# Cross attention with each step's projection piece ahead of its turn, VectorE's order changed to match, and the first norm moved into the loading block

## The reference, cut to what matters

```python
def _L0_attn_ref(x, ...):
    h = _ln(x, g1, beta1)                       # the "first norm"
    q = _phi((h @ wq).reshape(b, s, H, DH), proj)
    k = _phi((h @ wk).reshape(b, s, H, DH), proj)
    v = (h @ wv).reshape(b, s, H, DH)
    ...                                          # causal linear attention, wo, FFN
def _L0_xattn_ref(x, context, ...):
    xn = layer_norm(x, ...); cn = layer_norm(context, ...)
    q, k, v = xn @ Wq, cn @ Wk, cn @ Wv          # 16 heads of 64
    sim = einsum('bhid,bhjd->bhij', q * scale, k)     # 112 x 375 for each head
    attn = softmax(where(mask, sim, neg))
    out = einsum('bhij,bhjd->bhid', attn, v) @ Wo
x = _layernorm(x + _L0_attn_ref(x, ...))
x = _layernorm(x + _L0_xattn_ref(x, ctx, ...))
x = _layernorm(x + _L0_ffn_ref(x, ...))
```

## Time and profile before

| | |
|---|---|
| median of 3 runs | 2275.87 us |
| profiled execution, its own time | 2277.0 us |
| its span, first to last instruction | 2275.3 us |
| mean granted TensorE clock | 0.982 |
| busy: PE, PEld, DVE, ACT, POOL | 96%, 72%, 67%, 61%, 34% |
| layer 1, cross attention, layer 3 | to about 770, 770 to 2000, from 2000 us |

### The profile page before, as it was taken

How to read it: one execution, slowest core, us unless ns; L and a number is a source line. 1 busy time by engine, 2 the same in 40 slices (tenths; PEclk the granted TensorE clock), 3 DMA queues, 4 the chain that set the end, 5 groups by cost and what they waited for, 6 DMA issues and landing times. The chain is left out here.

```text
span 2275.3 us, 57835 instructions
## 1 busy us (share of the span) xinstructions
PE 2182.2 (96%) x20778; PEld 1640.8 (72%) x20778; DVE 1519.3 (67%) x4396; ACT 1380.3 (61%) x3178; POOL 762.4 (34%) x1335
## 2 busy tenths in 40 slices
PE   5999999999998999999999999999999999989997
PEld 4766867867867667777777777767677777868886
DVE  4555445545547677777777777777777777465647
ACT  5556356356354476767676767676767676544534
POOL 1122212212215244545444445454545454200003
PEclk8999999999999999999999999999999999789999
DMA  4100000000001100000000000000000000043202
GB/s 133 47 1 1 0 0 0 0 0 0 15 0 57 35 16 10 16 10 16 10 16 10 16 11 15 12 14 13 13 14 12 16 3 2 1 113 112 74 1 65
DMA packets 45732, 51.44 MB, mean 23 GB/s; under 512 B 19120, under 2 KB 37664, under 8 KB 45504
## 3 DMA queue, kind: packets, MB, share of 16 engines
q1 hardware_dynamic: 45504, 48.45, 7.2%
HBM read 44.78 MB, written 3.67 MB: 21 GB/s over the span
## 5 line engine op out<-in xcount | busy, mean ns | idle before, releaser
L1727 POOL TENSOR_SCALAR arena<-arena,p_rec 112x375 f32<-112x375 f32 x512 | 304.6, 596 | 617.3 <-DVE p_rec L1593 616.9
L64 PE MATMUL b_pb<-arena 128*125 128x512 f16 (+1 forms) x1364 | 379.9, 299 | 1.5 <-DVE k_lo L1564 1.5
L66 PE MATMUL b_pb<-arena 128*125 128x512 f16 (+1 forms) x1364 | 377.5, 298 | 0.0
L65 PE MATMUL b_pb<-arena 128*125 128x512 f16 (+1 forms) x1364 | 377.1, 297 | 0.0
L1597 DVE TENSOR_TENSOR pt_lo<-b_t,pt_hi 125x336 f16<-125x336 f32 x512 | 256.5, 501 | 140.7 <-ACT pt_hi L1488 140.7
L1579 DVE CUSTOM_DVE_ANT_0 arena<-b_s,arena 112x375 f32<-112x375 f32 x512 | 275.0, 537 | 100.6 <-PE b_s L1339 87.4
L1482 ACT ACTIVATE arena<-arena,neg_max 112x375 f32<-112x375 f32 x512 | 308.1, 602 | 1.4 <-DVE neg_max L1579 1.4
L1488 ACT ACTIVATE pt_hi<-b_t 125x336 f16<-125x336 f32 x512 | 226.9, 443 | 107.3 <-PE b_t L1348 107.2
L1348 PE MATMUL b_t<-ident,arena 112*125 112x112 f32 x1536 | 274.9, 288 | 12.3 <-POOL arena L1727 12.3
L1348 PEld LDWEIGHTS b_t<-ident,arena 112*125 112x125 f32 x1536 | 215.9, 190 | 71.0 <-POOL arena L1727 27.3
L952 POOL TENSOR_SCALAR_AFFINE_SELECT sm<-sm 112x448 f32<-112x448 f32 x128 | 72.0, 586 | 420.9 <-ACT sm L632 420.9
(11 more groups left out here) (279 smaller groups left out, 5726.0 us busy)
## 6 DMA issues: line engine op xcount, KB each, us to landing
arena<-in_L_ffn_W_dram SPq DMA_DIRECT2D x16, 1024.0 KB, 7.4
arena<-in_ctx_dram SPq DMA_DIRECT2D x32, 375.0 KB
out_dram<-c_z SPq DMA_DIRECT2D x8, 448.0 KB, 3.2
x_sb<-in_x_dram SPq DMA_DIRECT2D x1, 3136.0 KB, 18.8
ff<-in_L_attn_w_dram SPq DMA_DIRECT2D x2, 1024.0 KB, 6.8
ff<-in_L_xattn_Wkv_dram SPq DMA_DIRECT2D x2, 1024.0 KB, 5.3
arena<-in_mask_BxS_bf_dram SPq DMA_DIRECT2D x32, 41.0 KB, 2.6
a_raw<-in_L_attn_wq_dram SPq DMA_DIRECT2D x1, 1024.0 KB, 5.1
```

What stands on the lines that cost most here:

```text
L64: pe.matmul(out, lh, rh, start=first, stop=False)
L65: pe.matmul(out, lh, rl, start=False, stop=False)
L66: return pe.matmul(out, ll, rh, start=False, stop=last)
L1727: pool.tensor_scalar(p32[:, h % 4, :], p32[:, h % 4, :], p_rec[:, h % 4:h % 4 + 1], 0.0, ALU.mult, ALU.add).then_inc(p_norm_done, 1)
```

## The change

In cross attention the piece goes ahead of the turn on TensorE, and `piece_high` ahead of `turned_high` on ScalarE. On VectorE `turned_low` moves behind `sum_reciprocal`, and on odd steps behind `mask_max` as well. The last sequence, which has no pieces, keeps its order on TensorE and ScalarE. In the loading block x moves ahead of wk in the SyncE queue, wq and wk get semaphores of their own so that the transposes of wq need not wait for wk, and statistics, reciprocal root and rows of the first norm are made there.

```diff
 # layer1, main block, vector:
-            for b in range(G4):
-                ln_stats(0, b, x_rows(0)).then_inc(stats_done[0], 1)
-            ln_moments(0, 0)
-            for b in range(G4):
-                ln_rows(0, 0, b, x_rows(0), xh_rows)
             ln_low(0, 0)
             split_low(0)
 # layer1, main block, gpsimd:
-            ln_rstd(0, 0)
             pool.memset(v1[:, :, :, 0:DH], 0.0).then_inc(pads_done, 1)
 # load_layer1, sync:
             for i, n in enumerate(("L0_attn_wq", "L0_attn_wk")):
-                sp.dma_start(raw[i][:, :, :], rows(a[n])).then_inc(raw_loaded, 16)
+                sp.dma_start(raw[i][:, :, :], rows(a[n])).then_inc(raw_loaded[i], 16)
+                if i == 0:
+                    sp.dma_start(x_sb[:, 0:G4, :], ...).then_inc(x_loaded, 16)
             sp.wait_ge(p2_zero, 1)
...
-            sp.dma_start(x_sb[:, 0:G4, :], ...).then_inc(x_loaded, 16)
...
-            sp.wait_ge(x_loaded, 16)
 # load_layer1, gpsimd, behind ident:
+            settle(pool, passed, (mom_done, 1))
+            pool.tensor_scalar(rstd[:, 0, :], mom[:, 0, :, 1], EPS, None, ALU.add).then_inc(eps_done, 1)
+            pool.wait_ge(eps_done, 1)
+            pool.tensor_tensor(rstd[:, 0, :], rstd[:, 0, :], half_neg[0:T, :], ALU.pow).then_inc(rstd_done, 1)
 # load_layer1, tensor:
-            pe.wait_ge(raw_loaded, 32)
             for n in range(NT):
                 w, m2 = divmod(n, KI // 2)
+                if m2 == 0:
+                    pe.wait_ge(raw_loaded[w], 16)
 # load_layer1, vector, ahead of the fold's low parts:
+            dve.wait_ge(x_loaded, 16)
+            for b in range(G4):
+                dve.bn_stats(stats[:, 0, b, :], x_sb[:, b, :]).then_inc(stats_done, 1)
+            settle(dve, passed, (stats_done, G4))
+            for b in range(G4):
+                ins = dve.bn_aggr(mom[:, 0, b, :], stats[:, 0, b, :])
+            ins.then_inc(mom_done, 1)
+            dve.wait_ge(rstd_done, 1)
+            for b in range(G4):
+                ins = dve.tensor_scalar(xh[:, b, :], x_sb[:, b, :], mom[:, 0, b, 0:1], rstd[:, 0, b:b + 1], ALU.subtract, ALU.mult)
+            ins.then_inc(rows_done, 1)
 # layer2, tensor:
                 for s in range(H):
-                    turn_scores(b, s)
                     if not is_last(b):
                         piece(b + 1, 1 - par, s)
-                    else:
+                    turn_scores(b, s)
+                    if is_last(b):
 # layer2, scalar:
-                    turned_high(b, s)
                     if not is_last(b):
                         piece_high(b + 1, 1 - par, s)
-                    else:
+                    turned_high(b, s)
+                    if is_last(b):
 # layer2, vector:
-                    turned_low(b, s)
                     if s + 2 < H:
                         sum_reciprocal(b, s + 2)
                     elif not is_last(b):
                         sum_reciprocal(b + 1, s + 2 - H)
+                    if s % 2 == 0:
+                        turned_low(b, s)
                     if s + AHEAD < H:
                         mask_max(b, par, s + AHEAD)
                     elif not is_last(b):
                         mask_max(b + 1, 1 - par, s + AHEAD - H)
+                    if s % 2 == 1:
+                        turned_low(b, s)
```

More of the change, by code:

```diff
@@ L191, in layer1 @@
         b2 = sb("a_b2", [T, D], F32)
-        load_layer1(nc, a, x_sb, ident, half_neg, consts_done, hi, lo, (g1, be1, g2, be2, b1, b2), sb_in, psum_in, sem)
+        LNS = 3
+        xh = sb("xh", [T, G4, D], F32)
+        stats = sb("a_stats", [T, LNS, G4, 6], F32)
+        mom = sb("a_mom", [T, LNS, G4, 2], F32)
+        rstd = sb("a_rstd", [T, LNS, G4], F32)
+        norm_sems = [[sem(f"a_{n}{i}") for i in range(LNS)] for n in ("stats_done", "mom_done", "eps_done", "rstd_done", "rows_done")]
+        load_layer1(nc, a, x_sb, ident, half_neg, consts_done, hi, lo, (g1, be1, g2, be2, b1, b2),
+                    (xh, stats, mom, rstd), [sems[0] for sems in norm_sems], passed, sb_in, psum_in, sem)
         def pair(name, k, c0, n, width):
@@ L199, in layer1 @@
         FT = FF // P
-        LNS = 3
         NSM = 4
-        xh = sb("xh", [T, G4, D], F32)
         h32 = sb("h32", [P, KD, GT], F32)
@@ L222, in layer1 @@
         late = ("wv", "wo", "w1", "w2")
-        stats = sb("a_stats", [T, LNS, G4, 6], F32)
-        mom = sb("a_mom", [T, LNS, G4, 2], F32)
-        rstd = sb("a_rstd", [T, LNS, G4], F32)
         NPB = 4
@@ L347, in layer1 @@
         pb_free = [sem(f"a_pb_free{i}") for i in range(NPB)]
-        stats_done, mom_done, eps_done, rstd_done, rows_done = (
-            [sem(f"a_{n}{i}") for i in range(LNS)] for n in ("stats_done", "mom_done", "eps_done", "rstd_done", "rows_done"))
+        stats_done, mom_done, eps_done, rstd_done, rows_done = norm_sems
         h_hi_done = [sem(f"a_h_hi_done{i}") for i in range(2)]
@@ L1034, in _, with load_layer1 @@
             ln_rstd(NG - 1, 2)
-def load_layer1(nc, a, x_sb, ident, half_neg, consts_done, hi, lo, vectors, sb_in, psum_in, sem):
+def load_layer1(nc, a, x_sb, ident, half_neg, consts_done, hi, lo, vectors, norm, norm_sems, passed, sb_in, psum_in, sem):
     stack = ExitStack()
@@ L1042, in load_layer1 @@
         g1, be1, g2, be2, b1, b2 = vectors
+        xh, stats, mom, rstd = norm
+        stats_done, mom_done, eps_done, rstd_done, rows_done = norm_sems
         raw = [sb(f"a_raw{i}", [P, KD, INNER], F32) for i in range(2)]
@@ L1047, in load_layer1 @@
         fold_ps = [psum(f"a_fold{i}", [P, 4 * P]) for i in range(4)]
-        raw_loaded, vec_loaded, x_loaded = sem("a_raw_loaded"), sem("a_vec_loaded"), sem("a_x_loaded")
+        raw_loaded = [sem(f"a_raw_loaded{i}") for i in range(2)]
+        vec_loaded, x_loaded = sem("a_vec_loaded"), sem("a_x_loaded")
         p2_zero, p2_loaded = sem("a_p2_zero"), sem("a_p2_loaded")
@@ L1058, in _ @@
             for i, n in enumerate(("L0_attn_wq", "L0_attn_wk")):
-                sp.dma_start(raw[i][:, :, :], rows(a[n])).then_inc(raw_loaded, 16)
+                sp.dma_start(raw[i][:, :, :], rows(a[n])).then_inc(raw_loaded[i], 16)
+                if i == 0:
+                    sp.dma_start(x_sb[:, 0:G4, :], a["x"][0:G4, :, :].rearrange("b t d -> t b d")).then_inc(x_loaded, 16)
             sp.wait_ge(p2_zero, 1)
@@ L1062, in _ @@
                 sp.dma_start(proj2[DH * r:DH * (r + 1), DH * r:DH * (r + 1)], a["L0_attn_proj"]).then_inc(p2_loaded, 16)
-            sp.dma_start(x_sb[:, 0:G4, :], a["x"][0:G4, :, :].rearrange("b t d -> t b d")).then_inc(x_loaded, 16)
             for t, n in ((g1, "g1"), (be1, "beta1"), (g2, "g2"), (be2, "beta2"), (b1, "b1")):
```

## The result

The changed kernel takes 2253.23 us (median of four, 2248.58 to 2260.7) against 2276.03 for the kernel before: ratio 0.9887, 95% interval 0.986 to 0.9914. That is 22.8 us, where 39 had been forecast; it lies inside the range of 2222 to 2260 and on the side that had the chance of 0.93.

The account below looks back on a forecast made before the run. TensorE, busy 196.9 of 200 us in cross attention, was taken to set the pace. Loop -26 (-0.87 in thirty sequences), layer's first turn -2.2 and beginning -11.4 made -39.6 from 2277.0; forecast 2237 us, range 2222 to 2260.

Parts of the forecast that it names:

- The beginning and the layer's first turn: Loading block: first turn and first phi sooner, -11.4 us; layer's first turn: a piece fills its GpSimd wait, -2.2 us.
- The turn of step 8: Cross attention, TensorE: a piece covers the wait for GpSimd's normalise and the turn is no longer cold, -0.60 us a sequence.
- The seven other cold turns: Cross attention, TensorE: turns behind scores or values now stand behind a piece, -0.35 us a sequence (0 to -0.70).
- Scores behind a turn: Cross attention, TensorE: eight scores start sooner behind a turn than behind a piece, 0.02 us each, -0.16 a sequence.
- Scores that wait for mask_max: Cross attention, step 2: VectorE's turned order on odd steps brings the mask 0.4 us forward, -0.21 us a sequence.
- (b): VectorE: pieces 11 and 12 need piece_low of 9 and 10; just fits; +0.05 us together with (c).
- (a): ScalarE, step 14: x_columns, now behind turned_high, frees piece 15's bank late, so piece 15 waits +0.40 us a sequence.
- (c): GpSimd: step 9's normalise, queued behind the context's rows, comes due 0.6 us sooner; just fits; +0.05 together with (b).
- Rival 1: Cross attention: new bank waits of 1.2 us a sequence rather than 0.45 take the loop's gain, 2259 us; chance 0.2.
- Rival 3: Cross attention: the four values wait 0.4 us each for turned_low, making the kernel slower, 2284 us; chance 0.04.
- Rival 4: Beginning: clock stays low or wk is late, gaining 8 us instead of 11.4, 2240 us, inside the forecast; no own chance.
- Rival 2: Cross attention: changes of work cost less and x_columns is in time, -1.91 us a sequence, 2205 us; chance 0.08.

Follow-up runs that it names:

- experiment 2: Kernel before with only the first norm moved into the loading block, cross attention's order as before: 2267.46 us, ratio 0.996 (twelve runs).
- experiment 3: Kernel before with only the new order of cross attention, loading block as before: 2261.19 us, ratio 0.993 (six runs).
- experiment 6: Changed kernel with VectorE's out_low behind piece_low in step 9: 2242.95 us (one run).
- experiment 8: Changed kernel with out_low behind piece_low (step 9), x_columns first (step 14), piece_low of piece 14 in its own step: 2228.27 us, ratio 0.9773.
- experiment 1: Changed kernel run again with no edit: 2252.52 us (2246.49 to 2261.23, six runs), ratio 0.9886.
- experiment 5: Changed kernel with turned_low ahead of mask_max on every step, still behind sum_reciprocal: 2295.19 us (one run).
- experiment 4: Changed kernel with VectorE's old order, turned_low ahead of sum_reciprocal and mask_max: 2298.67 us (one run).
- experiment 7: Changed kernel with ScalarE's x_columns ahead of piece_high in step 14: 2259.82 us (one run).
- experiment 9: Experiment 8 plus 14 unread transposes on TensorE at the start of the last stage: 2228.1 us, ratio 0.9784 (five runs).

## Why the prediction was right, and where it failed

The direction was right and the size was not: 22.8 us of 39, inside the range because the range was wide. By the medians of experiments 2 and 3 the beginning gave 9.5 where 11.4 had been forecast, which is within its noise, and cross attention 15.8 where 28.2 had been.

**The beginning and the layer's first turn: right.** Forecast 11.4 and 2.2, together 13.6. In the profiled execution the first phi came 12.5 sooner and the first scores of layer 1 10.8; the start of layer 2 gave 2.4 (26.6 us from its first scores to its first output, now 24.2; experiments 6 and 8, which like the kernel before have the clock at 0.50 for 6.8 us there, show 24.7, so 1.9 is the order's and the rest the clock's). The loading block ends 2.6 sooner, not 1.5. Here the execution was lucky: wk was there at 10.5 as forecast (10.1), but its 16 turns took 1.97 and not half of 6.29, as they also do in experiment 2; in experiments 1, 6 and 8 they took 3.67 or 3.68, and the main block began at 23.4 to 23.8, a microsecond later than the forecast 22.4. The norm fits between x's landing (7.58) and the fold's first low part at 14.04, as said. The load of wv is late as said, but it is not what the first phi waits for; it acts through the loads behind it, and that the wait for w1 would take 1.7 back was not foreseen.

**The gains of the loop: the sum right, its terms not.** Without the new waits the forecast was -1.32 a sequence; the kernel without them (experiment 8) shows 36.343 - 37.700 = -1.36. By terms:

- The turn of step 8: forecast -0.60 with its own cold turn. The wait is gone and the piece ahead of it takes 1.30 to the turn instead of 1.81, -0.51; with the turn's 0.10, -0.61. Right.
- The seven other cold turns: forecast -0.35, the middle of 0 and -0.70. They save 0.10 each, and the pieces that now stand behind scores or values pay much less: 0.05 for a V piece (two), 0.01 for a K piece. That is about -0.56: the term was too small, since the middle was taken where the two kinds of work differ.
- Scores behind a turn: forecast -0.16, measured 0. A turn takes 0.41 to the scores and 0.32 to a piece, so scores still cost 0.09 more, exactly what they cost behind a piece before (1.39 against 1.30). The Trainium skill, TensorEngine Tiling (Array Packing), section Key Properties, says that changing the tiling mode drains TensorE. The trace agrees as to the time, scores start 0.09 late behind either kind of work; that a drain is the cause no row shows. The one row of layer 1 from which I took 0.05 has a different count of transposes and was no good measure.
- Scores that wait for mask_max: forecast -0.21, measured -0.28 (piece 2 takes 0.96 to 0.97 to the next start; before, 1.33, of which 0.09 were the change of work). But mask_max's new place does more than this term says: experiment 5 shows that without it the change would have made each sequence 0.8 us longer than before (38.502 against 37.700), and experiment 4, without sum_reciprocal's new place as well, 1.1. I had counted it as a gain of its own and not as what keeps the rest of the change alive.
- Not foreseen: a turn behind a Q piece, whose products are short, starts its successor later (0.47 to the scores, not 0.41; 0.37 to out_rows, not 0.32), +0.12 together. So two signs that the prediction gives for the profile did not come true as stated: turns ahead of scores and out_rows do not take 0.32, and three waits for mask_max are left.

**The step that failed: the new waits, (b).** Forecast +0.45, of which 0.40 for (a) and 0.05 for all of (b) and (c). Measured +0.85 (37.197 - 36.343): (a) is there with +0.35, and behind it +0.08 before the next sequence's piece 0; piece 10 waits +0.39 for piece_low of piece 8; some 0.03 are spread over other pieces. The kind of wait was named, a piece whose bank VectorE frees late, but I looked at pieces 11 and 12 alone and let "it just fits" stand. For piece 10 the chain has out_low in it, 0.62 us and ScalarE's b_o_hi ahead of it, and it had 0.08 to spare before the change, which makes TensorE's work in that time 0.42 shorter. Experiment 6 shows it: with these two exchanged the sequence is 0.394 shorter. In 30 sequences the waits took 0.40 x 30 = 12.1 more than forecast and the other terms gave 0.04 x 30 = 1.1 more, so the loop gave 15.1 us instead of 26. In the profiled execution it gave 14.0: 28 of the sequences between its two points are 0.50 shorter each, and the others, of which the last run partly at the lower clock in both kernels, give nothing together. For the whole execution: -39.6, -1.0 (a better beginning), +12.0 (the loop, 14.0 for 26), +8.4 (behind the loop) make -20.2.

**The rivals.** Rival 1, new waits of 1.2 a sequence instead of 0.45, was half right: 0.85. Rival 3 (values wait for turned_low) did not come: values are at the same distances as before, and no wait of that kind stands in the list. Its neighbour, scores waiting for mask_max, would have come with VectorE's old order. Rival 4 (the clock stays low or wk is late, 8 us instead of 11.4) came in part: in experiments 1, 6 and 8 the wk turns took twice as long, and the first turn was at 23.4 to 23.8 and not 21.3. Experiment 2, 9.5 us over twelve runs, lies between it and the forecast. Rival 2 asked for -1.91 a sequence; even without any new wait it is -1.36, since the third term gives nothing.

**The last 8.4 us** are not the change's work. 7.6 of them are the clock in the last stage of one execution, as experiment 1 shows with 64.1 us at the full clock; the other 0.8, ahead of that stage, were not traced. The medians have such executions on both sides: in experiment 1 they are 24.5 apart, and so are the fastest of each, 2246.49 and 2270.86 (24.4).

## What to carry to other kernels

When work is moved ahead in a ring of banks, list for every user of the ring who frees the bank that it needs and what stands ahead of that on its queue, for all steps and not only for those that look tight; here one step of sixteen had an extra instruction in the chain and cost 0.39 of the 1.36 us that the loop had to give. A new wait that is removed can give nothing until the one behind it is removed too, as experiment 7 shows, so read the distances from start to start after each fix. And where executions of one kernel differ by more than the change, compare the period of the loop from the timeline: it was 37.197 in both profiles of the changed kernel, while layer 1 differed by 11 us between them and the last stage by 8.

## What the runs showed of the hardware

- The granted clock fell to 0.50 at different places in executions in which this stretch of code was the same: behind the experts (changed kernel, 71.7 us for a stage of 64.1; experiment 7, 73.4), in layer 1 (experiments 1 and 9, 708.9 us for 698 to 703), and in neither in experiments 2 and 3. The idle time ahead of the last stage was the same 1.4 us in the kernel before, where the clock stayed at 1.00.
- A float16 piece loses 0.01 us behind values (K pieces, 0.97 instead of 0.96) and 0.05 behind scores (V pieces, 1.35 instead of 1.30), where three float32 transposes lose 0.10 behind either. Whether the piece's shape or the work ahead of it makes the difference between 0.01 and 0.05 no run separates; the one Q piece behind scores loses 0.01.
- Four rows of the norm took 1.38 us in the loading block and 6.23 beside GpSimd's memsets. In the changed kernel the memsets run at 21.26 to 26.5, and h_lo of VectorE in the midst of them, at 23.29, took 0.63, as it did before the change at 37.43, behind them. So the memsets do not slow every operation of VectorE; which kinds they slow was not tried.
